# A ring of six gathered tiles instead of five, with the edges' table and early constants in the bias row's place

## The chip, the cores and the metric

The kernel runs on one core of one Trainium2 chip. The metric is the device time of one execution in microseconds, the median of several. The engines are named as in the profile: PE is TensorE, DVE is VectorE, ACT is ScalarE, POOL is GpSimd, SP is SyncE. All on-chip tensors (SBUF) have 128 partitions; PE writes into eight banks of PSUM (`ps`).

## The reference, cut to what matters

A gated relational graph layer with a normalised input, N = 1250 nodes, D = 1024 features, R = 8 relations and 20000 edges:

```python
h = jnp.maximum(_layernorm(x, axis=-1), 0.0)
# _rgcn(h, ...): msgs = h[src]
out = h @ root + bias
for r in range(8):
    mask = (edge_type == r)
    sums = segment_sum(msgs * mask[:, None], dst, num_segments=n)
    cnt = segment_sum(mask, dst, num_segments=n)
    out = out + (sums / maximum(cnt, 1.0)[:, None]) @ weight[r]
# the gate, with u = out
z = concatenate([u, h], axis=1) @ w_gate + b_gate
result = x + tanh(u) * z + h * (1.0 - z)
```

## The kernel before

The kernel multiplies first and sums afterwards. For each relation it forms y = h @ weight[r] for all nodes and stores the rows in memory off the chip (`y_rows`). Then it gathers, for each edge, the row of its source and relation, and sums the rows of the edges with the same destination by a product with a one-hot matrix. Numbers are split into a high and a low half of 16 bits, so each product of a block is three matmuls, and a row of `y_rows` holds 2 x 1024 halves (4 KB).

**The products.** All work of PE hangs on a count n of products (`for n in range(NU)`), each written to one of four banks of `ps`. The eleven weights are eight relations, root, and the two halves of w_gate. The first three take 20 products each in the plain way; from the fourth on the kernel uses seven products of quarter size for eight (`winograd(n)`, 35 per weight), and the last half of w_gate is plain again. Every engine walks through the same n in its own program, with what is due at each n written out in tables: conversions of the next weight (L765 on ACT, L1001 and L1017 on DVE), evacuations (L1123), stores and loads on SP.

**The groups and their tiles.** The edges are put into 80 groups, one for each relation and each block of 125 destinations. Early in the run (n up to 32) DVE computes each edge's place in a table of tiles of 128 edges, POOL scatters the edges into the table (L624, 160 DMAs), loads it back (L628), and DVE unpacks it into `edges` at n = 109 (`table()`). A group has at least two tiles. The groups are worked through in four sweeps, of relations 0 to 2, 3 and 4, 5 and 6, and 7. A sweep begins at a multiple of RING in the table: `group_bounds()` rounds the tiles of each sweep up to whole turns of the ring, and the last group of a sweep takes the tiles that are left over, which hold no edge. Their gathers name a row beyond the bound and move nothing.

**The ring.** `G` is a ring of RING gathered tiles of 128 x 2048 halves (4 KB per partition each), in the tensor `early`. POOL fills it. Its program for tile t is `make_onehot(t - LAG)`, then `columns(t + 1)`, then the gather of tile t (L651): the one-hot tile of t - 3 waits until that gather has landed, and the gather of t waits until PE has summed tile t - RING (`onehot_free`). So with LAG = 3 at most three gathers are in flight, and at the end of a sweep POOL makes the last three one-hot tiles (L687) before it begins the next sweep.

**The sums.** PE takes the first tile of group g at product `AGG_AT[g]` and the others one product later (`REST_AT`), from n = 113 on. A tile is four matmuls of 128x512 (L1330), for the high and low halves of both halves of the row, and one small one that counts (L1333). DVE divides the sum by the count and adds it to a block of u (`add_group`, L1202 to L1212) in one of three buffers `ub`, which SP stores to and loads from `u_rows` between sweeps. PE may begin the next group when DVE has added this one (`u_added`).

**Other places that the diff touches.** `early` also holds, at other times, the layer norm's buffers (`xbuf`, `hbuf`, `hilo`), the operand sums of the quarter-size products (`sbuf_s`, read until `s_low`), weight half C and the bias row `brow`, which DVE first reads when the root weight begins (n = 235). `weight_top` spreads a weight's maximum over 128 columns (`wspread`, L979), for PE to transpose.

## Time and profile before

| what | before |
|---|---|
| three timed runs | 1382.66, 1378.94, 1381.46 us |
| median | 1381.46 us |
| the profiled execution | 1374.83 us |
| its span | 1373.1 us |
| mean granted clock of PE | 0.989 |
| DMA, read from and written to memory | 203.66 MB and 87.30 MB |

The profile is of one execution, which is 6.63 us shorter than the median. An engine's busy time is what its instructions took; the idle time in front of an instruction is put down to the one that released it. The chain that ended last has PE for 61% of the span, DVE for 13%, DMA for 9% and issue for 9%. The first tile is summed at 501 us and the last at 1138 us.

### The profile page before, as it was taken

The page shows a single profiled execution, that of the slowest core. Times are in us where ns is not written, and L with a number is a line of the kernel's source. Part 1 is how long each engine was busy: PE and PEld are TensorE (multiplying, and loading weights), DVE is VectorE, ACT ScalarE, POOL GpSimd, SP SyncE. Part 2 cuts the span into 40 slices and gives each one's busy share as a digit, 9 for nine tenths or more (in the row PEclk, how much of TensorE's full clock was granted, in tenths as well). Part 3 has the DMA queues.
Part 4 walks back from the last instruction along what each step waited for, and adds up shares of the span by engine and source line. Part 5 has one row for each costly group of instructions (what it writes and reads, how often), then busy time and mean ns, then how long its engine had stood idle before and what let it go on. Part 6 is the DMA issues. An engine that isn't in the chain of part 4 may idle for free.

```text
span 1373.1 us, 20220 instructions
## 1 busy us (share of the span) xinstructions
PE 1280.7 (93%) x6207; PEld 646.9 (47%) x6207; DVE 953.5 (69%) x1296; ACT 425.4 (31%) x526; POOL 785.5 (57%) x880
## 2 busy tenths in 40 slices
PE   3899999999999999999998999999999889979998
PEld 1445444444444444445454445444445444434665
DVE  6879897476556747766684567556585657787886
ACT  4472223244325414320331132222311111575200
POOL 6222078787878746776787676866685644331000
PEclk9999999999999999999999999999999999998999
DMA  6371133251144268676775978588787996677876
GB/s 226 134 274 62 43 115 116 54 175 47 30 132 115 53 219 261 188 210 236 249 218 166 301 268 280 191 295 280 223 267 238 343 311 188 189 255 217 250 222 209
DMA packets 112474, 269.43 MB, mean 196 GB/s; under 512 B 22678, under 2 KB 23181, under 8 KB 112388
## 3 DMA queue, kind: packets, MB, share of 16 engines
q1 hardware_dynamic: 75204, 175.63, 38.6%
q0 software_dynamic: 37184, 92.64, 23.3%
q8 instruction: 55, 0.90, 0.3%
q14 instruction: 31, 0.25, 0.1%
HBM read 203.66 MB, written 87.30 MB: 212 GB/s over the span
## 4 chain that ended last, share of the span: by engine, by line
PE 61%; DVE 13%; DMA 9%; issue 9%; ACT 4%; POOL 3%; POOLq 0%; DVEq 0%; SPq 0%; ACTq 0%
PE ps L1368 51%; PE ps L1330 10%; DMA early<-y_rows,pair 6%; DMA early<-u_rows 2%; POOL onehot L659 2%; DVE W L1001 2%; DVE hT L1049 1%; DMA W<-in_L_gnn_weight_dram 1%; ACT W L765 1%; POOL early L651 1%; DVE wspread L979 1%; DVE yhl L1123 1%; DVE early L1212 1%; DVE yhl L1134 1%; DVE hT L1054 1%
## 5 line engine op out<-in xcount | busy, mean ns | idle before, releaser
L1368 PE MATMUL ps<-W,hT 128*128 128x512 f16 (+2 forms) x4740 | 1066.0, 382 | 12.8 <-DVE W L1001 8.2
L1368 PEld LDWEIGHTS ps<-W,hT 128*128 128x128 f16 (+2 forms) x4740 | 475.8, 103 | 528.2 <-issue 22.9
L624 POOL DMA_INDIRECT table_rows<-edges,table_i x160 | 245.3, 1533 | 112.4 <-issue 112.4
L651 POOL DMA_INDIRECT early<-y_rows,pair x200 | 234.6, 1173 | 105.3 <-PE ps L1333 62.4
L1330 PE MATMUL ps<-early,onehot 128*125 x800 | 207.6, 387 | 41.1 <-POOL onehot L659 21.6
L659 POOL TENSOR_SCALAR onehot<-iota_d,pair 128x125 f16<-128x125 f16 x188 | 152.9, 813 | 87.6 <-DMA early<-y_rows,pair 80.7
L1330 PEld LDWEIGHTS ps<-early,onehot 128*125 x800 | 106.8, 137 | 117.0 <-issue 68.2
L815 ACT ACTIVATE yhl<-early 128x512 f16<-128x512 f32 x100 | 62.8, 628 | 319.7 <-DVE early L1123 183.0
L1001 DVE SCALAR_TENSOR_TENSOR W<-W,wsc 128x2048 f16<-128x2048 f32 x62 | 148.3, 2393 | 16.4 <-ACT W L765 16.4
L765 ACT ACTIVATE W<-W,wsc 128x2048 f16<-128x2048 f32 x62 | 122.7, 1991 | 105.3 <-DVE W L1017 51.6
L732 ACT ACTIVATE peek_out<-W 128x1024 bf16<-128x1024 f32 x80 | 84.2, 1053 | 135.1 <-DMA W<-in_L_gnn_weight_dram 63.3
L1212 DVE SCALAR_TENSOR_TENSOR early<-ps,inv,early 125x1024 f32<-125x1024 f32 x70 | 89.9, 1284 | 2.4
L807 ACT ACTIVATE yhl<-ps 128x512 f16<-128x512 f32 (+1 forms) x60 | 35.7, 594 | 168.7 <-PE ps L1368 155.4
L1100 DVE SCALAR_TENSOR_TENSOR yhl<-ps,yhl 128x512 f16<-128x512 f32 (+1 forms) x60 | 40.6, 684 | 52.3 <-ACT yhl L807 45.6
L1202 DVE TENSOR_SCALAR inv<-ps,wsc 125x1 f32<-125x1 f32 x80 | 17.2, 216 | 75.8 <-PE ps L1333 65.9
L1088 DVE TENSOR_TENSOR yhl<-early,yhl 128x512 f16<-128x512 f32 x100 | 68.8, 688 | 0.7 <-ACT yhl L815 0.5
L1123 DVE SCALAR_TENSOR_TENSOR early<-ps,Q 128x512 f32<-128x512 f32 x50 | 34.5, 689 | 48.9 <-PE ps L1368 45.2
L598 POOL TENSOR_TENSOR early<-early 128x1024 f16<-128x1024 f32 (+1 forms) x10 | 27.2, 2724 | 70.8 <-ACT early L780 70.8
L1017 DVE TENSOR_TENSOR W<-W 128x2048 f32<-128x2048 f32 x26 | 61.1, 2351 | 0.1
L1123 DVE SCALAR_TENSOR_TENSOR early<-ps,hT 128x512 f32<-128x512 f32 x50 | 34.4, 689 | 36.5 <-PE ps L1368 30.5
L641 POOL COPY pair<-edges 128x2 int32 x200 | 56.5, 283 | 3.6 <-POOL onehot L687 1.9
L1123 DVE SCALAR_TENSOR_TENSOR Q<-ps,Q 128x512 f32<-128x512 f32 x50 | 34.2, 684 | 26.8 <-PE ps L1368 26.8
(191 smaller groups left out, 851.4 us busy)
## 6 DMA issues: line engine op xcount, KB each, us to landing
y_rows<-yhl SPq DMA_DIRECT2D x144, 256.0 KB
W<-in_L_gnn_weight_dram SPq DMA_DIRECT2D x30, 1024.0 KB
u_rows<-early SPq DMA_DIRECT2D x50, 448.0 KB
early<-u_rows SPq DMA_DIRECT2D x30, 448.0 KB
W<-in_L_gnn_w_gate_dram SPq DMA_DIRECT2D x8, 1024.0 KB
early<-in_x_dram SPq DMA_DIRECT2D x9, 512.0 KB, 4.8
hs_rows<-early SPq DMA_DIRECT2D x9, 512.0 KB, 4.1
root_rows<-yhl SPq DMA_DIRECT2D x18, 256.0 KB
```

The source lines that it names most:

```text
L624: pool.indirect_dma_start(out=table_rows, out_offset=bass.IndirectOffsetOnAxis(ap=at_i[:, c:c + 1], axis=0), in_=packed[0:EP, c:c + 1], in ...
L651: pool.indirect_dma_start(out=G[:, b, :], out_offset=None, in_=y_rows[i], in_offset=bass.IndirectOffsetOnAxis(ap=idx[:, b, :], axis=0), bo ...
L659: pool.tensor_scalar(onehot[:, b, 0:DT], iota_d[:, :], dcol[:, b, :], None, ALU.is_equal).then_inc(s["tile_ready"], 1)
L732: nc.scalar.activation(peek_out[:, :], homes[LAND[w][q]][:, half * D:(half + 1) * D], ACT.Abs, accum_out=wsum[:, w, 2 * q + half:2 * q + h ...
L765: nc.scalar.activation(Wv[MAT[w][c]][:, 0, :], homes[at], ACT.Copy, scale=wscale(w, 0, c // 2)).then_inc(s["w_hi"], 1)
L815: nc.scalar.activation(yhl[:, o % 4, 0, :], C[:, o % 2, :], ACT.Copy).then_inc(s["y_hi"], 1)
L1001: nc.vector.scalar_tensor_tensor(out=Wv[MAT[w][c]][:, 1, :], in0=homes[at], scalar=wscale(w, 0, c // 2), in1=Wv[MAT[w][c]][:, 0, :], op0=A ...
L1088: nc.vector.tensor_tensor(yhl[:, o % 4, 1, :], C[:, o % 2, :], yhl[:, o % 4, 0, :], ALU.subtract).then_inc(s[YDONE], 1)
L1123: return nc.vector.scalar_tensor_tensor(out=to, in0=part, scalar=scale, in1=of, op0=ALU.mult, op1=ALU.add)
L1212: nc.vector.scalar_tensor_tensor(out=ub[0:DT, b, :], in0=sums, scalar=inv[0:DT, 1:2], in1=ub[0:DT, b, :], op0=ALU.mult, op1=ALU.add).then_ ...
L1330: nc.tensor.matmul(ps[0:DT, 4 + half, :], hot_t, rows[:, bass.ds(ring_slot * (2 * D) + (half * D + part * HC), HC)], start=first and part ...
L1368: last = nc.tensor.matmul(ps[0:rows, n % 4, :], hT[:, m, v_h, k, n0:n0 + rows], Wh[MAT[w][c]][:, v_w, k, :], start=(first and v_h + v_w == ...
```

## The change

RING is 6 instead of 5, and the table is 348 columns wide instead of 345, a multiple of 6. `early` gets an eleventh block of 1024 columns, so the ring lies in blocks 1 to 6, the three buffers `ub` in blocks 7 to 9 and the bias row in block 10. The edges' table `table_i`, the group offsets `tb`, `before`, `ones_bf`, `groups`, `ltile` and `iota_g`, all of them used only before the first sweep, lie in the bias row's block until the table is unpacked. The bias row is therefore loaded at n = 133 instead of n = 10, behind a wait for `table_ready`. `ones_f` has 8 columns instead of 128, and the spread of the maximum and the helper copies at a sweep's end read other tensors. Slot 5 of the ring is cleared by a memset of its own, behind a wait for `s_low`.

```diff
--- before.py
+++ after.py
@@ -28,9 +28,9 @@
     DT = 125
     NJ = N // DT
     NG = R * NJ
-    RING = 5
+    RING = 6
     LAG = 3
-    TMAX = 345
+    TMAX = 348
     HC = 512
     HT = 5
     KH = 4
@@ -247,19 +247,21 @@
         Q = sb("Q", [P, HT, HC], F32)
         yhl = sb("yhl", [P, 4, 2, HC], F16)
         peek_out = sb("peek_out", [P, D], BF16)
-        early = sb("early", [P, 10 * D], F32)
+        early = sb("early", [P, 11 * D], F32)
         edges = sb("edges", [P, TMAX, 2], I32)
-        table_i = sb("table_i", [P, TMAX], I32)
-        tb = sb("tb", [P, NG], F32)
         ident = sb("ident", [P, P], F32)
         ident_h = sb("ident_h", [P, P], F16)
-        ones_f = sb("ones_f", [P, P], F32)
-        ones_bf = sb("ones_bf", [P, P], BF16)
-        before = sb("before", [P, P], BF16)
-        groups = sb("groups", [NG, NG + NS], BF16)
+        ones_f = sb("ones_f", [P, 8], F32)
+        at_brow = early[:, 10 * D:11 * D]
+        table_i = at_brow[:, 0:TMAX].bitcast(I32)
+        before, ones_bf, ltile = (at_brow[:, TMAX + i * P // 2:TMAX + (i + 1) * P // 2].bitcast(BF16) for i in range(3))
+        ltile = ltile[0:NG, :]
+        tb = at_brow[:, TMAX + 3 * P // 2:TMAX + 3 * P // 2 + NG]
+        groups = at_brow[0:NG, TMAX + 3 * P // 2 + NG:TMAX + 3 * P // 2 + NG + (NG + NS) // 2].bitcast(BF16)
+        iota_g = at_brow[:, TMAX + 3 * P // 2 + 2 * NG:TMAX + 3 * P // 2 + 3 * NG]
+        assert (NG + NS) % 2 == 0 and (NG + NS) // 2 <= NG and TMAX + 3 * P // 2 + 3 * NG <= D
         ones_h = sb("ones_h", [P, 2], F16)
         iota_d = sb("iota_d", [P, DT], F16)
-        iota_g = sb("iota_g", [P, NG], F32)
         pair = sb("pair", [P, RING, 2], I32)
         onehot = sb("onehot", [P, RING, P], F16)
         bounds = sb("bounds", [P, NG + 1], I32)
@@ -267,7 +269,6 @@
         turn_f = sb("turn_f", [P, 4, NS + 1], F32)
         tstart = sb("tstart", [P, NG], F32)
         ntile = sb("ntile", [NG, 4], F32)
-        ltile = sb("ltile", [NG, P], BF16)
         warm = sb("warm", [P, 1], F32)
         held = sb("held", [P, LAG * NS], F32)
         stats = sb("stats", [P, 2, 2, 6], F32)
@@ -302,9 +303,9 @@
         hbuf = early[:, 4 * D:6 * D].rearrange("p (b n) -> p b n", b=2)
         hilo = early[:, 6 * D:8 * D].bitcast(F16).rearrange("p (b n) -> p b n", b=2)
         sbuf_s = early[:, 6 * D:8 * D].rearrange("p (m k n) -> p m k n", m=4, k=KH)
-        G = early[:, D:6 * D].bitcast(F16).rearrange("p (b n) -> p b n", b=RING)
-        ub = early[:, 6 * D:9 * D].rearrange("p (b n) -> p b n", b=3)
-        brow = early[:, 9 * D:10 * D]
+        G = early[:, D:7 * D].bitcast(F16).rearrange("p (b n) -> p b n", b=RING)
+        ub = early[:, 7 * D:10 * D].rearrange("p (b n) -> p b n", b=3)
+        brow = early[:, 10 * D:11 * D]
         brow_gate = early[:, 0:D]
         uhl = [G[:, b, :] for b in (0, 1)]
         root_in = [G[:, b, :].bitcast(F32) for b in (2, 3)]
@@ -498,7 +499,8 @@
                     if r == 23:
                         sp.wait_ge(s["w_lo"], conv_no(w, 6) + 1)
                         land(w + 1, 3)
-                if n == 10:
+                if n == AGG_AT[0] + 20:
+                    sp.wait_ge(s["table_ready"], 1)
                     load_brow(brow, bias)
                 if n == unit(W_ROOT, 2, 0):
                     sp.wait_ge(s[YDONE], 2 * NJ * W_ROOT + 1)
@@ -628,8 +630,10 @@
             pool.dma_start(table_i[:, :], table_rows.rearrange("(p t) one -> p (t one)", p=P)).then_inc(s["table_loaded"], 16)
 
             pool.wait_ge(s["w_lo"], conv_no(PLAIN, 3) + 1)
+            pool.wait_ge(s["s_low"], HT)
             pool.memset(early[:, D:2 * D], 0.0).then_inc(s["ring_clear"], 1)
-            pool.wait_ge(s["ring_clear"], 2)
+            pool.memset(early[:, 6 * D:7 * D], 0.0).then_inc(s["ring_clear"], 1)
+            pool.wait_ge(s["ring_clear"], 3)
             pool.wait_ge(s["onehot_free"], RING)
             pool.wait_ge(s["tile_ready"], RING)
             pool.wait_ge(s["table_ready"], 1)
@@ -683,7 +687,7 @@
                     turn(i, q)
                 for b in range(RING - LAG, RING):
                     pool.wait_ge(s[f"gathered{b}"], q1 * 16)
-                    pool.tensor_tensor(held[:, LAG * i + b - RING + LAG:LAG * i + b - RING + LAG + 1], iota_g[:, 0:1], iota_g[:, 0:1], ALU.add)
+                    pool.tensor_tensor(held[:, LAG * i + b - RING + LAG:LAG * i + b - RING + LAG + 1], ones_f[:, 0:1], ones_f[:, 0:1], ALU.add)
                     pool.tensor_scalar(onehot[:, b, 0:DT], iota_d[:, :], dcol[:, b, :], None,
                                        ALU.is_equal).then_inc(s["tile_ready"], 1)
 
@@ -976,7 +980,7 @@
                 else:
                     dve.wait_ge(s["peeked"], 4 + 8 * w)
                     step(nc.vector.tensor_reduce(wtop[:, 0:1], wsum[:, w, :], AX.X, ALU.max))
-                nc.vector.tensor_scalar(wspread[:, :], ones_f[:, :], wtop[:, 0:1], None, ALU.mult).then_inc(s["wtop_ready"], 1)
+                nc.vector.tensor_scalar(wspread[:, :], ident[:, :], 0.0, wtop[:, 0:1], ALU.mult, ALU.add).then_inc(s["wtop_ready"], 1)
 
             def first_peek(q):
                 dve.wait_ge(s[f"w_landed{q}"], 16)
```

Two engines' orders change. On POOL, ahead of the first gather (the copy of `pair` is the last instruction before the sweeps), before:

```order
L616 MEMSET early 128x4096
L617 MEMSET onehot 128x2
L618 MEMSET onehot 128x2
L624 DMA table_rows<-edges,table_i 44160x1 x160
L628 DMA table_i<-table_rows 128x345
L631 MEMSET early 128x1024
L674 COPY pair<-edges 128x2
```

and now:

```order
L618 MEMSET early 128x4096
L619 MEMSET onehot 128x2
L620 MEMSET onehot 128x2
L626 DMA table_rows<-edges,early 44544x1 x160
L630 DMA early<-table_rows 128x348
L634 MEMSET early 128x1024
L635 MEMSET early 128x1024
L678 COPY pair<-edges 128x2
```

One memset is added ahead of the copy; the scatter and the load of the table go to `early` and have 348 columns. On SP, the bias row's load stood between the stores of the first weight's products (y_rows) and of the normalised rows (hs_rows), before:

```order
L416 DMA y_rows<-yhl 128x1024 x2
L399 DMA hs_rows<-early 128x1024
L402 DMA early<-in_L_gnn_bias_dram 128x1024
L416 DMA y_rows<-yhl 128x1024 x2
L399 DMA hs_rows<-early 98x1024
L416 DMA y_rows<-yhl 128x1024 x4
```

and now it stands between the stores of the first sweep (u_rows is the store of a finished block of sums):

```order
L417 DMA y_rows<-yhl 98x1024
L435 DMA u_rows<-early 112x1024
L435 DMA u_rows<-early 13x1024
L403 DMA early<-in_L_gnn_bias_dram 128x1024
L417 DMA y_rows<-yhl 128x1024
L435 DMA u_rows<-early 112x1024
L435 DMA u_rows<-early 13x1024
```

No other instruction of SP has moved. PE, DVE and ACT keep their order; the body of POOL's loop over the turns of the ring holds six tiles instead of five.

## Rows read from the trace of the kernel before

**Rows 1.** The page, part 1: busy us (share of span), instructions

```profile
PE 1280.7 (93%) x6207; PEld 646.9 (47%) x6207; DVE 953.5 (69%) x1296; ACT 425.4 (31%) x526; POOL 785.5 (57%) x880
```

**Rows 2.** Stretches: busy us (instructions) by engine, then granted clock, DMA share, GB/s

```profile
490.00:727.00 237.00, 226.33 (x1085) 115.26 (x1084) 159.00 (x252) 66.49 (x88) 170.85 (x227) 0.99 0.70 225
727.00:889.00 162.00, 150.46 (x721) 77.61 (x720) 99.78 (x141) 41.48 (x52) 115.24 (x160) 0.99 0.78 251
889.00:1051.00 162.00, 153.18 (x739) 78.83 (x738) 105.86 (x149) 36.83 (x42) 111.31 (x154) 0.99 0.81 258
1051.00:1139.00 88.00, 77.96 (x369) 39.57 (x368) 51.49 (x79) 15.10 (x19) 47.96 (x75) 0.98 0.94 310
```

**Rows 3.** Waits of PE, 490 to 1140 us: us, times, longest us

```profile
PE ps L1330 <- POOL onehot L659: 21.6, 19, 3.2
PE ps L1330 <- DVE early L1212: 10.6, 8, 3.9
```

**Rows 4.** Waits of POOL in the same stretch

```profile
POOL onehot L659 <- DMA early<-y_rows,pair: 80.7, 45, 5.3
POOL early L651 <- PE ps L1333: 62.4, 39, 3.3
...
POOL pair L674 <- DVE edges L1079: 8.1, 1, 8.1
```

**Rows 5.** Groups by line: the count matmul that closes each tile

```profile
L1333 PE MATMUL ps<-ones_h,onehot 128*125 128x2 f16 x200 | 33.5, 168 | 0.0
```

**Rows 6.** Timeline of PE, first to second sweep: start, us, instruction [idle before]

```profile
726.26 0.17 PE L1333 MATMUL ps<-ones_h,onehot 128*125 128x2 f16 x1
...
730.00 2.75 PE L1368 MATMUL ps<-W,hT 128*128 128x512 f16 x12
735.98 1.07 PE L1330 MATMUL ps<-early,onehot 128*125 x4 [3.23 <-POOL onehot L659]
...
738.21 1.96 PE L1330 MATMUL ps<-early,onehot 128*125 x4 [1.16 <-POOL onehot L659]
```

**Rows 7.** Timeline of PE, the ends of the second and the fourth sweep

```profile
887.49 1.06 PE L1330 MATMUL ps<-early,onehot 128*125 x4
...
889.33 5.34 PE L1368 MATMUL ps<-W,hT 128*128 128x512 f16 x24
...
1136.41 1.07 PE L1330 MATMUL ps<-early,onehot 128*125 x4
...
1137.53 1.07 PE L1330 MATMUL ps<-early,onehot 128*125 x4
```

**Rows 8.** Timeline of POOL, gathers before the first sweep's end

```profile
711.04 1.07 POOL L651 DMA_INDIRECT early<-y_rows,pair  x1 [0.62 <-POOL pair L641]
...
713.07 1.08 POOL L651 DMA_INDIRECT early<-y_rows,pair  x1 [0.16 <-issue]
...
718.36 1.07 POOL L651 DMA_INDIRECT early<-y_rows,pair  x1 [0.16 <-issue]
```

**Rows 9.** Timeline of POOL at 958 to 973 us, and of PE behind it

```profile
961.86 1.07 POOL L651 DMA_INDIRECT early<-y_rows,pair  x1 [1.48 <-PE ps L1333]
...
972.58 0.61 POOL L659 TENSOR_SCALAR onehot<-iota_d,pair 128x125 f16<-128x125 f16 x1 [5.25 <-DMA early<-y_rows,pair]
...
991.88 1.07 PE L1330 MATMUL ps<-early,onehot 128*125 x4 [2.22 <-POOL onehot L659]
```

**Rows 10.** Busy time by stretch, around one place of lower granted clock

```profile
727.00:737.00 10.00, 6.60 (x32) 3.50 (x30) 4.47 (x5) 0.63 (x1) 8.32 (x12) 1.00 0.44 119
737.00:742.00 5.00, 3.84 (x14) 1.87 (x13) 1.67 (x3) 0.00 (x0) 4.47 (x9) 0.66 0.57 177
```

**Rows 11.** Timeline, 98 to 104 us: the bias row's load

```profile
99.41 0.46 SPq L402 DMA_DIRECT2D early<-in_L_gnn_bias_dram  x1
```

**Rows 12.** Groups by line: the memset of one ring slot

```profile
L631 POOL MEMSET early<- 128x1024 f32 x1 | 1.0, 970 | 0.0
```

**Rows 13.** The instructions of L979: shortest/median/longest ns, first and last start

```profile
L979 DVE TENSOR_SCALAR wspread<-ones_f,wtop x12: 286/304/5092, 13.2 to 1231.2; 128x128 f32<-128x128 f32 x12
```

## The prediction, made before the changed kernel was run

> **What bounds the kernel now.** I read the page's busy times first, then the busy times by stretch, then the waits of PE and of POOL, and last the timeline around the ends of the sweeps. PE is busy 1280.7 us, 93% of the span of 1373.1 us [rows 1]. The stretches [rows 2] show where PE is not busy: the gathering, from 490 to 1139 us, has 649 us of which PE fills 607.9 us (226.33 + 150.46 + 153.18 + 77.96), so 41 us are idle there, and the DMA share rises from 0.70 to 0.94. In that stretch PE's idle time lies ahead of the summing matmuls of L1330 [rows 3]: 21.6 us until POOL's one-hot tile of L659, 10.6 us until DVE has added the group before (L1212). No plain product (L1368) waits there. So PE sets the time, interrupted by a ring of gathered tiles that is at times empty.
>
> Whether the ring has a slot too few is to be read from POOL [rows 4]. POOL waits 62.4 us in 39 waits for PE to free a slot (L651 on L1333), and 80.7 us in 45 waits for a gather to land (L659). Only the first kind is moved by a sixth slot. The second comes from having three gathers in flight (LAG stays 3) and from how long one takes.
>
> **Part 1, fewer tiles of nothing.** Each sweep starts on a multiple of RING, and the missing tiles are gathered, made one-hot and multiplied like real ones. All 200 show up [rows 5]. I counted the edges of the inputs by group: 71, 47, 47 and 23 real tiles in the four sweeps. Rounded to fives that is 75 + 50 + 50 + 25 = 200; rounded to sixes 72 + 48 + 48 + 24 = 192. So 8 tiles go, 3, 2, 2 and 1, each at the end of a sweep, where PE takes them one behind the other with no product between.
> - First sweep: the last padding tile that stays ends at 726.26 + 0.17 = 726.43 us, the product behind the other three starts at 730.00 us [rows 6]: 3.57 us.
> - Second: from 887.49 to 889.33 us, 1.84 us for two tiles [rows 7]. The third sweep has the same pattern, 1.84 us.
> - Fourth: one tile at the pitch from 1136.41 to 1137.53 us, 1.12 us [rows 7].
> Sum 8.4 us, all on PE, and PE has nothing beside it to hide them. The ends of the bounds: 0 if what follows each sweep waits for something else anyway, 8.4 us if not; I take 8.4 us, since the four places are solid PE.
>
> **Part 2, waits for a one-hot tile.** Of the 21.6 us [rows 3] the first tiles of the ring account for about 2.5 us: they wait for the table, not for a slot, and stay. That leaves 19.1 us.
> - At the start of the second sweep PE waits 3.23 + 1.16 = 4.39 us [rows 6]. POOL has no wait for PE between 711 and 728 us; it is busy with its own queue. From the gather at 718.36 us on, three in it are padding [rows 8], and each costs POOL at least the pitch of 2.03 us from 711.04 to 713.07 us, with its copy and its one-hot. POOL comes 6.1 us sooner, PE 3.57 us sooner, so 2.5 us of the 3.23 us go, and the 1.16 us behind it: 3.7 us. In the page this gain is not the sixth slot's but again the padding's.
> - Elsewhere one slot moves a gather that waited for PE forward by one tile of PE. From one summing to the next that is 3.48 us where one product lies between. An example [rows 9]: the gather issued at 961.86 us had waited 1.48 us for PE, and from there on POOL found no wait for PE until PE itself ran dry at 991.88 us for 2.22 us. An earlier lead of 3.48 us covers it. The other stalls outside the first sweep's end are of the same size or smaller (the longest is the 3.23 us above). I count 8.6 us for those between the ring's start and the end that stand directly behind a late one-hot tile; the other 6.1 us of the 19.1 us I leave, as waits that are put down to POOL while its tile had been ready.
> Sum 12.3 us; bounds 3.7 us (only the padding's) and 19.1 us (all).
>
> **Part 3, the clock.** The granted clock is 1.00 in the 10 us ahead of 737 us, in which PE was busy only 6.60 us, and 0.66 in the 5 us behind it [rows 10], which is a stretch at the lower level of 1.2 GHz inside one at 2.4 GHz. In it four summing matmuls took 1.96 us [rows 6], against 1.07 us in the row at 735.98 us. With the product behind them such a place costs about 1.5 us. If the wait ahead of it goes, so can this. There are three such places behind waits of the ring; I take two, 3.1 us, bounds 0 and 4.7 us.
> The Trainium skill, "TensorE: Matmul & The Clock Gate", What's actually happening, says that the clock follows how busy TensorE has been recently. The trace agrees, as far as one place shows it; by the rule all three would go, 4.7 us.
>
> **Part 4, what is given back.** The same bytes of gathers, loads and stores now fall into some 24 us less. That is 3.7% of 649 us, at a DMA share that is already 0.78 to 0.94 from 727 us on [rows 2]. The gather issued at 961.86 us had its one-hot at 972.58 us, after a wait of 5.25 us for the landing [rows 9], so within 10.7 us; 3.7% of this is 0.4 us, and I take 0.2 us as the other end, once for every three tiles in flight, so for about 41 of the 124 tiles behind the first sweep: 8 to 15 us at the worst, if every wait for landing reached PE. Most are absorbed by the ring. Bounds 0 and 15 us, I take 5 us. The bias row's load (512 KB, L402) moves from 99.41 us [rows 11] to product 133, near 570 us, where SP's queue holds it between stores and nobody is waiting for it before product 235. Its SP time is 0.46 us; its landing lies beside the gathers there. Bounds 0 and 3 us, I take 1 us. The wait for the table that now stands ahead of it on SP is over by 492 us.
>
> **Edits that I cost at nothing.** The second memset of a ring slot (0.97 us like the one before it [rows 12]) stands on POOL ahead of a wait of 8.1 us for DVE's table [rows 4]; without this cover it would cost 0.97 us. The wait for s_low in front of it is satisfied since product 56. The held copies, the smaller ones_f and the constants in the bias row keep shapes and engines. The spread of the weight maximum reads ident times 0 plus the maximum instead of ones times it: same width, one pass, 0.30 us in the median and at most 5.09 us [rows 13]. The two long ones, near 13 and 31 us, end when POOL's memsets end, whatever they read; bounds per instruction -0.05 and +0.1 us, so within 1 us for twelve.
>
> **Sum.** 8.4 + 12.3 + 3.1 - 5 - 1 = 17.8 us. The profiled execution took 1374.83 us and would take 1357 us. The median of the three timed runs is 1381.46 us, 6.6 us longer than the profiled one, and I take the sum from it: 1363.7 us.
>
> **Rivals.**
> - Only the padding goes: 8.4 + 3.7 us less, with 5 to 6 us given back: about 6 us, 1375 us. For it speaks that POOL's larger wait is for landings (80.7 against 62.4 us), which one slot doesn't shorten. Against it: after a wait for PE, each gather is issued earlier, and a lead once gained is kept until a late landing uses it.
>  The Trainium skill, "DMA: Bandwidth & Descriptors", Issuing engines are not separate DMA queues, says that all DMAs end on the same 16 engines and interleave there. By it a deeper ring buys lead and no bandwidth, so this rival's time follows. The DMA share of 0.94 [rows 2] agrees.
> - Everything that one can see goes: 8.4 + 19.1 + 4.7 us and nothing given back, 32 us; nearer to what has been seen, 27 us: 1354 us.
> - The gain is eaten behind the gathering: the last two weights, the loads of the sums or the final stage set the end by something that doesn't move with PE. Then 0 to 4 us remain, 1380 us. Against it: the chain behind 1139 us is PE and the weights' conversion, and both are released by PE's progress.
> - Slower: landings become the bound. With three in flight, each microsecond by which gathers land later delays 41 rounds, if it reaches PE. Gains of 23.8 us are used up from 0.6 us per gather on. At 0.8 us it is 33 us against 24 us, 9 us slower, 1390 us. Its place would be from 840 to 1110 us, where the DMA share is highest. Against it: the bytes don't grow, they shrink by none, and the loads keep their place in the order of products.
> - The change not doing what it says (no sixth tile, more padding) I hold excluded by the counts above.
>
> **Chances.** The forecast 0.47, only the padding 0.22, all of it 0.17, eaten behind 0.08, landings as the bound 0.06. A measurement of this kernel tells 0.3%, 4.1 us, from no change. Faster by more: 0.87 (forecast, all of it, nearly all of the padding case, and a part of the rest); within it 0.08; slower by more 0.05. The range from 1353 to 1377 us leaves out the last two cases and little else.
>
> **What would show it.** L1333 x192 instead of x200. PE's wait for L659 falls from 21.6 us to under 9 us, POOL's wait for L1333 grows, since POOL runs into the full ring more often. PE's busy time in summing falls by about 9 us. At the start of the second sweep the wait of 3.23 us is under 1 us. Fewer stretches at half clock between 490 and 1139 us. The first tile is summed at the same time, 501 us, and the gathering ends near 1120 us instead of 1139 us. It is wrong if the waits for landing (80.7 us) grow by more than the waits for a slot and PE's wait for L659 stays; if PE's wait for DVE (10.6 us) grows by 5 us or more; or if the time from the last summed tile to the end, 235 us now, becomes longer.

## The result, and the profile after

The changed kernel takes 1356.02 us in the median of four runs (1354.90 to 1360.29), the kernel before 1380.55 us (1378.94 to 1382.66) beside it. The ratio is 0.9839, 95% interval 0.9814 to 0.9864, which is 19 to 26 us less. The forecast was 1363.7 us, range 1353 to 1377: faster, as predicted, by 4 us more than the sum said when taken by the ratio (22 against 17.8 us).

The profiled execution took 1356.57 us, with a span of 1354.8 us; the one of before 1374.83 us with 1373.1 us. From one profile to the other it is 18.3 us. Part 1 of the page, to be read beside [rows 1]:

```profile
PE 1270.8 (94%) x6167; PEld 641.1 (47%) x6167; DVE 950.1 (70%) x1296; ACT 425.4 (31%) x526; POOL 775.5 (57%) x857
```

Groups by line, PE, to be read beside [rows 5]:

```profile
L1334 PE MATMUL ps<-early,onehot 128*125 x768 | 198.4, 385 | 34.1 <-DVE early L1216 13.3 <-POOL onehot L663 9.3 <-issue 7.8
L1337 PE MATMUL ps<-ones_h,onehot 128*125 128x2 f16 x192 | 32.1, 167 | 0.0
```

Lines have moved by four: L1330 is L1334 now, L1333 is L1337, L651 is L655, L659 is L663. PE counts 192 tiles. It is 9.9 us less busy, and its waits are down by 7 us. The sweeps in stretches, columns as in [rows 2]:

```profile
490.00:729.00 239.00, 228.90 (x1104) 116.65 (x1103) 162.05 (x256) 66.50 (x88) 172.82 (x232) 1.00 0.73 233
729.00:882.00 153.00, 146.70 (x711) 75.25 (x710) 101.97 (x145) 42.10 (x53) 108.88 (x146) 1.00 0.82 264
882.00:1038.00 156.00, 149.87 (x722) 76.76 (x721) 104.86 (x146) 36.21 (x42) 108.31 (x150) 0.99 0.85 269
1038.00:1122.00 84.00, 72.44 (x338) 36.71 (x337) 46.95 (x73) 15.09 (x19) 40.69 (x64) 0.96 0.91 301
```

From the first summing matmul of a sweep to that of the next, the sweeps last 225.7, 153.1, 156.3 and 84.2 us. Before, they were 234.5, 158.5, 161.2 and 82.9 us, the last one to its last tile in both. So 8.9, 5.4 and 4.9 us are gained in three sweeps, and the fourth is 1.2 us longer. This last difference tells nothing: two profiles of a ring of five, the kernel before and the first of the experiments, have 82.9 and 88.7 us there with the same 25 tiles. Outside the sweeps little moved. The first tile is summed at 502.9 us (501.4 before), and from the last tile to the end it is 232.6 us (234.5).

The waits of PE and POOL from 490 to 1125 us (us in total, times, longest us), to be read beside [rows 3, 4]:

```profile
PE ps L1334 <- DVE early L1216: 13.3, 9, 5.1
PE ps L1334 <- POOL onehot L663: 9.3, 9, 2.1
...
POOL onehot L663 <- DMA early<-y_rows,pair: 84.5, 48, 6.0
POOL early L655 <- PE ps L1337: 46.1, 27, 5.2
```

PE now waits for a one-hot tile 9 times, where it waited 19 times before (in a second profile of the same kernel, taken with the experiments, 13 times, 13.0 us). POOL waits less for PE, not more. At the start of the second sweep, where PE stood 3.23 and 1.16 us [rows 6], the timeline of PE (start, us, instruction) has no wait ahead of the first tile, and only the engine's own 0.95 us ahead of the second:

```profile
726.01 2.75 PE L1372 MATMUL ps<-W,hT 128*128 128x512 f16 x12
728.60 1.03 PE L1334 MATMUL ps<-early,onehot 128*125 x4
...
730.58 1.07 PE L1334 MATMUL ps<-early,onehot 128*125 x4 [0.95 <-issue]
```

The largest stall that is left lies in the last sweep, and it isn't the ring's. Timelines of DVE and PE there, and last the same stall of PE before the change:

```profile
1090.76 0.22 DVE L1206 TENSOR_SCALAR inv<-ps,wsc 125x1 f32<-125x1 f32 x1 [4.88 <-DMA early<-u_rows]
...
1085.04 2.75 PE L1372 MATMUL ps<-W,hT 128*128 128x512 f16 x12
1092.90 1.96 PE L1334 MATMUL ps<-early,onehot 128*125 x4 [5.11 <-DVE early L1216]
...
1108.75 1.07 PE L1330 MATMUL ps<-early,onehot 128*125 x4 [3.90 <-DVE early L1212]
```

DVE waits for the partial sums to be loaded back (u_rows), and PE waits for DVE. The tile behind it is summed at half clock (granted clock 0.50): 1.96 us in the place of 1.03. The DMA engines are nearly all busy in this stretch (third column from the end the granted clock, then their share). By windows:

```profile
1038.00:1060.00 22.00, 20.66 (x101) 10.53 (x100) 10.01 (x13) 6.20 (x9) 12.92 (x19) 1.00 0.99 322
1060.00:1080.00 20.00, 16.90 (x82) 8.29 (x79) 15.16 (x22) 2.70 (x5) 14.04 (x22) 1.00 1.00 344
1080.00:1100.00 20.00, 14.26 (x58) 6.91 (x59) 8.06 (x15) 2.30 (x4) 6.67 (x12) 0.83 0.97 336
```

### The profile page after: what moved, and what is told of

It reads as the page before. It is cut to its first block, busy times and chain, and to the rows that moved or that the text cites. A ratio compares the mean times of both kernels' runs of the same rounds, so it can differ in the third digit from the quotient of the medians.

```text
span 1354.8 us, 19982 instructions
## 1 busy us (share of the span) xinstructions
PE 1270.8 (94%) x6167; PEld 641.1 (47%) x6167; DVE 950.1 (70%) x1296; ACT 425.4 (31%) x526; POOL 775.5 (57%) x857
## 4 chain that ended last, share of the span: by engine, by line
PE 58%; DVE 13%; DMA 10%; issue 9%; ACT 4%; POOL 4%; POOLq 1%; SPq 0%; DVEq 0%; ACTq 0%
PE ps L1372 49%; PE ps L1334 9%; DMA early<-y_rows,pair 6%; POOL onehot L663 2%; DVE W L1005 2%; DMA early<-u_rows 2%; DVE hT L1053 1%; POOL early L655 1%; DMA W<-in_L_gnn_weight_dram 1%; ACT W L769 1%; DMA u_rows<-early 1%; DVE wspread L983 1%; ACT hT L847 1%; ACT peek_out L736 1%; DVE early L1216 1%
## 5 line engine op out<-in xcount | busy, mean ns | idle before, releaser
L626 POOL DMA_INDIRECT table_rows<-edges,early x160 | 248.2, 1551 | 114.6 <-issue 114.6
L655 POOL DMA_INDIRECT early<-y_rows,pair x192 | 228.7, 1191 | 86.5 <-PE ps L1337 46.1
L1334 PE MATMUL ps<-early,onehot 128*125 x768 | 198.4, 385 | 34.1 <-DVE early L1216 13.3
L663 POOL TENSOR_SCALAR onehot<-iota_d,pair 128x125 f16<-128x125 f16 x180 | 151.6, 842 | 90.1 <-DMA early<-y_rows,pair 84.5
L1005 DVE SCALAR_TENSOR_TENSOR W<-W,wsc 128x2048 f16<-128x2048 f32 x62 | 148.1, 2390 | 16.9 <-ACT W L769 16.9
L1334 PEld LDWEIGHTS ps<-early,onehot 128*125 x768 | 102.4, 137 | 107.5 <-issue 59.3
L736 ACT ACTIVATE peek_out<-W 128x1024 bf16<-128x1024 f32 x80 | 84.2, 1053 | 139.1 <-DMA W<-in_L_gnn_weight_dram 64.0
L1092 DVE TENSOR_TENSOR yhl<-early,yhl 128x512 f16<-128x512 f32 x100 | 69.1, 691 | 0.7 <-ACT yhl L819 0.5
L1021 DVE TENSOR_TENSOR W<-W 128x2048 f32<-128x2048 f32 x26 | 60.9, 2342 | 0.1
L645 POOL COPY pair<-edges 128x2 int32 x192 | 47.3, 246 | 5.1 <-issue 4.2
```

The lines of the kernel that those rows point to most:

```text
L626: pool.indirect_dma_start(out=table_rows, out_offset=bass.IndirectOffsetOnAxis(ap=at_i[:, c:c + 1], axis=0), in_=packed[0:EP, c:c + 1], in ...
L655: pool.indirect_dma_start(out=G[:, b, :], out_offset=None, in_=y_rows[i], in_offset=bass.IndirectOffsetOnAxis(ap=idx[:, b, :], axis=0), bo ...
L663: pool.tensor_scalar(onehot[:, b, 0:DT], iota_d[:, :], dcol[:, b, :], None, ALU.is_equal).then_inc(s["tile_ready"], 1)
L736: nc.scalar.activation(peek_out[:, :], homes[LAND[w][q]][:, half * D:(half + 1) * D], ACT.Abs, accum_out=wsum[:, w, 2 * q + half:2 * q + h ...
L1005: nc.vector.scalar_tensor_tensor(out=Wv[MAT[w][c]][:, 1, :], in0=homes[at], scalar=wscale(w, 0, c // 2), in1=Wv[MAT[w][c]][:, 0, :], op0=A ...
L1092: nc.vector.tensor_tensor(yhl[:, o % 4, 1, :], C[:, o % 2, :], yhl[:, o % 4, 0, :], ALU.subtract).then_inc(s[YDONE], 1)
```

## The experiments

The first theory was the prediction's: padding costs PE's time, a slot buys lead, and both add up. The rivals were that the gain comes from the layout, that the price of padding is POOL's, and that landings set the pace. Each kernel was timed in five rounds against the kernel before; the times are medians, and the ratios are to the kernel before in the same set of runs. A difference of two ratios is uncertain by about 0.004, 6 us.

### The layout and the late bias row alone

```diff
 (kernel after)
-    RING = 6
+    RING = 5
     LAG = 3
-    TMAX = 348
+    TMAX = 345
...
-        G = early[:, D:7 * D].bitcast(F16).rearrange("p (b n) -> p b n", b=RING)
+        G = early[:, D:6 * D].bitcast(F16).rearrange("p (b n) -> p b n", b=RING)
```
Everything else of the change stays, the second memset and the wait in front of it too; the block that this memset clears is then no slot of the ring.

> The changed kernel with five slots and 345 columns again; the table in the bias row's place, the bias row loaded late, the extra memset and wait, and the spread from ident all stay. My theory (fewer padding tiles and one slot more are the whole gain): 200 tiles again, 1380 us, within 0.3% of before. Rival (the table's place, the late bias row or the other small edits carry a part): clearly below 1376 us, at the extreme 1356 us.

1379.26 us beside 1379.47 us, ratio 1.0001 (0.9978 to 1.0025). The shared place, the bias row's load at product 133, the second memset and the other spread together cost and bring nothing that this can tell, that is nothing over some 3 us. So the gain is the ring's.

### Six slots, five in use

```diff
 (kernel after, gather)
-                pool.wait_ge(s["onehot_free"], t + 1)
+                pool.wait_ge(s["onehot_free"], t + 2)
```

> The changed kernel with six slots and 192 tiles, but a gather waits for one more tile to be summed, so that only five slots are ever in use. It takes the depth away and leaves the padding at 192. My theory: the padding is worth 8.4 + 3.7 = 12 us and the slot the rest, so about 1367 us (between 1363 and 1371). Rival 1 (only the padding counts): 1356 us. Rival 2 (only the slot counts): 1380 us. PE's wait for the one-hot tile: 10 to 17 us by my theory, 9 us by rival 1, 21 us by rival 2.

1367.03 us, ratio 0.9899 (0.9874 to 0.9925). With 192 tiles and the old depth 14 us are gained (10 to 17), and the sixth slot in use brings the other 8 us (0.9899 against 0.9839). The waits of PE in this kernel:

```profile
PE ps L1334 <- POOL onehot L663: 22.6, 19, 2.8
PE ps L1334 <- DVE early L1216: 9.4, 6, 3.6
```

The time is the one that my theory gave (1367 us), but the wait is not: 10 to 17 us were expected, and the 22.6 us in 19 waits are those of [rows 3], as if only the slot counted for them. Leaving out padding hardly shortens them; the slot does.

By sweep, this kernel takes 226.8, 158.7, 159.1 and 82.1 us in its profile. Against the kernel before, nearly all of the padding's gain lies in the first sweep (7.8 us for three tiles), and the two tiles that went from the second brought nothing that one profile shows; 14 us for eight tiles is an average. Against the kernel after, the sixth slot in use brings 5.5 us in the second sweep and 2.8 us in the third (5.8 us and nothing against that kernel's second profile). The start of the second sweep on PE's timeline:

```profile
729.97 1.03 PE L1334 MATMUL ps<-early,onehot 128*125 x4
...
733.76 1.07 PE L1334 MATMUL ps<-early,onehot 128*125 x4 [2.77 <-POOL onehot L663]
```

Without the padding and with the old depth the 3.23 us ahead of the first tile [rows 6] are gone, but the second tile waits 2.77 us in the place of 1.16. So 1.6 us of the 4.39 us go with the padding, and the others only with the sixth slot.

### Four slots in use

```diff
 (kernel after, gather)
-                pool.wait_ge(s["onehot_free"], t + 1)
+                pool.wait_ge(s["onehot_free"], t + 3)
```

> The kernel after (192 tiles) with gathers held back until two more slots are free, so that four of its six slots are used at a time. It draws the curve of the ring's depth at an equal number of tiles: with five of six in use the time was 1367.0, with six 1356.0 (8 to 11 us for the sixth slot). If each slot buys its 3.5 us of lead at every tile that is late, the fifth bought more than the sixth: four slots 1390 to 1415 us, ratio 1.007 to 1.025, and TensorE waits 40 to 70 us for one-hots (23 with five, 9 with six). If the gain of the sixth came by other ways (the layout, the clock), four would stand near five, 1367 to 1372 us.

1384.68 us, ratio 1.0029 (1.0008 to 1.0051). At 192 tiles the ratios for four, five and six slots in use are 1.0029, 0.9899 and 0.984: the fifth slot was worth 18 us, the sixth 8 us. The time came out under the 1390 us expected, and so did PE's wait for one-hots, 33.7 us in 34 waits and not 40 to 70 us.

### Padding tiles passed by PE, ring of five

```diff
 (kernel before, tensor engine, loop over a group's tiles)
-                with pe.Fori(t0 + 1, t1) as t:
+                with pe.Fori(t0 + 1, tr) as t:        # tr: end of the real tiles
                     sum_tile(t, False)
+                with pe.Fori(tr, t1) as t:            # padding: the counting matmul alone
+                    pass_tile(t)
```

> The kernel before, five slots and 200 tiles, but PE passes the 12 padding tiles with the small counting matmul alone, without the four summing matmuls (they add nothing to the sums). POOL still gathers and makes all 200. My theory: 12 x 0.9 us less on PE, a part of it lost because POOL's 2 us per padding tile stays and PE then waits at the start of the next sweep: 6 us less, 1374 us. Rival (a padding tile costs by PE's matmuls alone): 11 us less, 1369 us. Rival (it costs by POOL alone): no change, 1380 us.

1381.12 us, ratio 1.0003 (0.9984 to 1.0023). This told most against my theory, which had 1374 us; the rival that a padding tile costs by POOL alone had 1380 us. Some 10 us of PE's work are gone (the summing matmuls of 12 padding tiles, estimated from their 0.86 us each) and the time is the same. PE and POOL in this kernel, the same stretch:

```profile
PE ps L1333 <- POOL onehot L660: 28.9, 24, 4.6
...
POOL early L652 <- PE ps L1336: 76.7, 46, 4.0
POOL onehot L660 <- DMA early<-y_rows,pair: 64.6, 40, 6.0
```

PE waits 7.3 us more for one-hots than in [rows 3]. What it saves on padding it waits for POOL, which still has to gather it and make it one-hot.

### 24 more padding tiles

```diff
 (kernel after, group_bounds)
-    step(nc.vector.tensor_scalar(turn_f[:, 0, 0:NS], turn_f[:, 1, 0:NS], -ROUND, None, ALU.add))
+    step(nc.vector.tensor_scalar(turn_f[:, 0, 0:NS], turn_f[:, 1, 0:NS], -ROUND + 1.0, None, ALU.add))
```

> The kernel after with one more turn of its ring of six in each sweep: 24 more padding tiles, 216 tiles in all. It asks what a padding tile costs. If it is TensorE's own time, as the prediction had it, 24 x 1.05 us (the summing matmuls of one tile) = 25 us, 1381 us, ratio to the kernel before 1.002. If it is GpSimd's time, 24 x 2.04 us (gather, columns and one-hot of one padding tile) = 49 us, and nothing of it hidden, 1405 us, ratio 1.02; with the six tiles of the ring's lead hidden at each of four sweep ends, between the two. From the run with a ring of six of which five are used (8 tiles fewer than before, 13.9 us faster of 1380) I expect 1.7 us for each, 41 us: 1397 us, ratio 1.014. TensorE's wait for one-hots would rise from 9.3 us to over 25 by GpSimd's theory, and stay under 12 by TensorE's.

1404.8 us, ratio 1.0170 (1.0142 to 1.0198), against 0.984: 45 us for 24 tiles, 1.9 us each. That is near POOL's price (2.04 us), not PE's (1.05 us), with next to nothing hidden; 1397 us, 1.7 us each, had been expected. PE's wait for L663 rose to 24.5 us, just short of "over 25".

### The same, passed by PE

The edits of the last two together, on the kernel after.

> The same 216 tiles, and TensorE passes each padding tile with its counting matmul alone, so that a padding tile costs it some 0.1 us in the place of 1.05. Against the run with the 24 more padding tiles: if a padding tile's price is TensorE's work, 28 x 0.9 = 25 us of it go and the kernel is at 1355 to 1370 us; if it is GpSimd's, nothing goes (within 3 us of that run, near 1397 us) and TensorE's wait for one-hots rises by some 15 to 25 us in its place.

1406.7 us, ratio 1.0192 (1.0164 to 1.0220): nothing is gained by taking some 25 us from PE. Its waits for one-hots are 50.4 us in the place of 28.9 us with the padding summed, L691's (here L692's) included, so 21.5 us of them came back as waiting. The timelines of PE (L1346 is the counting matmul of a padding tile) and of POOL at the end of the first sweep:

```profile
727.45 0.21 PE L1346 MATMUL ps<-ones_h,onehot 128*125 128x2 f16 x1 [0.84 <-POOL onehot L664]
729.48 0.21 PE L1346 MATMUL ps<-ones_h,onehot 128*125 128x2 f16 x1 [1.82 <-POOL onehot L664]
...
725.52 1.09 POOL L656 DMA_INDIRECT early<-y_rows,pair  x1 [0.16 <-issue]
726.65 0.62 POOL L664 TENSOR_SCALAR onehot<-iota_d,pair 128x125 f16<-128x125 f16 x1
727.22 0.18 POOL L646 COPY pair<-edges 128x2 int32 x1
727.56 1.07 POOL L656 DMA_INDIRECT early<-y_rows,pair  x1 [0.17 <-POOL pair L646]
```

PE runs 0.21 us and stands 1.82 us, and its pitch of 2.03 us is that of POOL's three instructions, 1.07 to 1.09 us for the gather, 0.62 for the one-hot, 0.18 for the copy, and the gaps. Nothing of it waits for a landing here.

### Four gathers in flight

```diff
 (kernel after)
-    LAG = 3
+    LAG = 4
```

> The changed kernel with four gathers in flight instead of three (LAG 4), six slots as they are. POOL's waits for landings were 84 us in 48 waits. If they bound the gathering (the rival that landings are the bound), PE's wait for the one-hot tile falls from 9 us to under 4 us and the time by 5 us or more, under 1351 us. My theory: with six slots they are covered, the time stays within 3 us of 1356 us, and one tile less of finished lead may cost as much as it gives.

1357.04 us, ratio 0.9845 (0.9807 to 0.9882), the kernel after within its scatter. But POOL's waits change place:

```profile
POOL early L655 <- PE ps L1337: 139.5, 79, 7.2
```

In the kernel after it waited 84.5 us for landings and 46.1 us for slots. Here the one-hots wait 6.8 us for landings, and POOL waits for slots in their place. So the waits for landing are for the most part slack that shows up at one wait or the other. One reserve stays: the fourth gather in flight also means one finished tile less ahead of PE, and a gain and a loss that cancel would look the same. PE's wait for L663 hardly changed (8.6 us against 9.3).

### One more operation of GpSimd for each tile

```diff
 (kernel after, columns)
                 pool.tensor_copy(pair[:, b, :], eflat[:, bass.ds(t * 2, 2)]).then_inc(s["idx_ready"], 1)
+                pool.tensor_tensor(extra[:, b:b + 1], ones_f[:, 0:1], ones_f[:, 0:1], ALU.add)
```

The kernel after ran in the same set:

> The kernel after, unchanged, on the chip of the two kernels beside it, so that they can be read against it: 1354 to 1360 us, ratio 0.981 to 0.986.

It took 1357.75 us, ratio 0.9845 (0.9815 to 0.9875).

> The kernel after with one more operation of GpSimd for each gathered tile, an addition over one column (194 ns in the trace, some 0.25 us with its issue), behind the columns of the next tile: 192 x 0.25 = 48 us more of GpSimd's work between 490 and 1122 us. If GpSimd's own pace sets these sweeps, most of it shows: 1390 to 1404 us. If GpSimd's time counts only where no real tile is being summed (the padding tiles, 12 or so of 192, and the fill of the ring at four sweeps, 4 x 3 tiles), it is 24 x 0.25 = 6 us or less, 1356 to 1364 us, and its waits for TensorE (46 us) and for landings (84 us) shrink by what is added.

1368.83 us, ratio 0.9933 (0.9906 to 0.9960), 11 us more than the kernel after beside it. A tile takes POOL 2.21 us from gather to gather, where it took 2.04, 33 us in 192 tiles, and its busy time on the page is 34.0 us more than that of the kernel after beside it (810.1 against 776.1). Neither theory had it: a third of POOL's added time shows, where the one said nearly all and the other that of at most 24 tiles of 192. The wait that grew is PE's for the one-hot, 13.0 us in the kernel after of this set:

```profile
PE ps L1336 <- POOL onehot L665: 24.7, 16, 4.7
```

By sweep, 225.5, 157.5, 159.4 and 88.1 us stand against 225.6, 152.8, 159.3 and 83.7 us: in these two profiles the first and the third sweep hide POOL's added time, the second and the fourth don't.

### The load of u_rows one product earlier

```diff
 (kernel after, sync engine, loop over k)
+                    if n == STEP_END[k] + 1 and NJ <= k + 2 < len(STEPS):
+                        load_u(k + 2)
                     if n == STEP_END[k] + 2:
                         store_u(k)
-                        if NJ <= k + 2 < len(STEPS):
-                            load_u(k + 2)
```

> The kernel after with the load of the partial sums u_rows for a group two steps on issued one product earlier and ahead of the store that it stood behind. In the trace of the kernel after VectorE waits 4.9 us for such a load at 1090 us and TensorE 5.1 us behind it, with one stretch of 6.8 us at half clock. If SyncE's order is what makes that load late, the wait goes: 5 us of wait and up to 1.7 us of clock, 1349 to 1353 us, ratio 0.978 to 0.981 to the kernel before. If the load is late because the DMA engines are full there (0.97 to 1.00 of their time in these 60 us), the gathers land later in its place, and nothing is gained: 1355 to 1358 us, ratio 0.983 to 0.985.

1352.42 us, ratio 0.9794 (0.9762 to 0.9826), and once more, beside the kernel after:

> The kernel with the load of u_rows issued earlier once more, now beside the kernel after. Its first timing gave a ratio of 0.9794, 6 us under that of the kernel after in another set of runs, but its profile still has a wait of 6.4 us in the last sweep, on the same kind of load, and half-clock stretches in other places. If the gain is the edit's, it is again 3 to 8 us under the kernel after: 1349 to 1354 us. If it was the scatter between sets of runs, the two agree within 2 us.

1353.49 us, ratio 0.9823 (0.9790 to 0.9856), 4.3 us under the kernel after. Both sets point the same way, by 3 and 6 us by their ratios, but the intervals overlap with those of the kernel after. It is the fastest kernel here; that it beats the kernel after is likely and not shown. The times are those of my theory, but the reason that I gave fails, since the wait was to go. PE in its first profile:

```profile
1090.77 1.96 PE L1334 MATMUL ps<-early,onehot 128*125 x4 [6.37 <-DVE early L1216]
```

DVE's wait for the same kind of load is still there (4.6 us). In the second profile PE waits 6.4 us for DVE at the same place, but there the profile puts only 1.6 us of DVE's waits down to this load. That the load is late because the DMA engines are full would fit the first profile and is not shown. What shortened the second and third sweeps (by 1.9 and 3.8 us in the first profile) stays open.

### The wide operations of DVE in halves

```diff
 (the kernel with the earlier load, low_weights; sum_quadrants in the same way)
-                nc.vector.scalar_tensor_tensor(out=Wv[MAT[w][c]][:, 1, :], in0=homes[at], ...
+                for m in range(2):
+                    k = slice(m * 1024, (m + 1) * 1024)
+                    part = nc.vector.scalar_tensor_tensor(out=Wv[MAT[w][c]][:, 1, k], in0=homes[at][:, k], ...
```

> The kernel with the earlier load of u_rows, and VectorE's two widest operations on the weights (the low part L1005 and the sum of quadrants L1021, 128x2048, 2.3 us each) written as two of 1024 columns. In the trace of the kernel after, 39 gathers, one-hots and copies of GpSimd take up to 3 us in the place of 0.2 to 1.1 us while one of these runs, 50 us in all, and end a fixed 0.96, 0.48 or 0.04 us behind its end. If GpSimd is shut out until the wide operation ends, and gets in between the halves, the longest of its gathers falls from 3.1 to about 2.2 us, its lost time falls from 68 us to 35 to 45 us, and, with a third of GpSimd's time reaching TensorE as the kernel with the extra operation showed, the time falls by 8 to 11 us, to 1342 to 1346 us, ratio 0.972 to 0.975. If GpSimd does not get in between two operations that follow each other at once, the lost time stays and the time is 1351 to 1355 us, ratio 0.979 to 0.983, or 1 to 2 us more for VectorE's 100 or so added instructions.

1358.49 us, ratio 0.9849 (0.9823 to 0.9876): no gain where 8 to 11 us were expected, and some 5 us more than without the halves, about what two sets of runs can differ by. What it says of POOL stands in the last section. POOL's time lost in stretched gathers, one-hots and copies (counted there) fell by 12.7 us (67.7 to 55.0), less than expected, and nothing of that reached the end. The sweeps are as long as with whole operations (152.6 and 152.8 us for the second and third, 151.2 and 152.5 with whole ones). POOL waits 75.6 us for slots where it waited 44.0. DVE is 16 us busier, and the part behind the last tile is 4.8 us longer, 239.0 us, so this kernel doesn't tell what less contention alone is worth.

## Why the prediction was right, and where not

**What bounds the kernel.** PE's summing, interrupted by a ring that runs dry: right. The slots in use show it directly, four to six at the same tiles.

**Part 1, 8.4 us "all on PE", with "nothing beside it to hide them".** The size was near and the place wrong. Fewer padding tiles are worth 14 us (10 to 17). The prediction had 8.4 us here, 3.7 us at the second sweep's start and about 1.5 us for the clock there, 13.6 us in all. But PE's matmuls of padding are worth nothing: with them left out the time stays, in a ring of five and with 28 padding tiles in a ring of six. PE's time and POOL's are not added up at a sweep's end. PE takes the padding quickly and then waits for the next sweep's first tile, which stands behind the padding in POOL's queue. The price is 1.9 us a tile on POOL. The prediction saw that queue in [rows 8] and used it for 3.7 us only, where it should have carried the whole term: eight times 1.9 us is 15 us. Even so it is an average, since by the profiles most of it came in the first sweep.

**Part 2, one slot elsewhere 8.6 us.** Right: the step from five to six in use is 8 us, though by a difference that is itself uncertain by 6 us. The wait of PE for one-hots fell from 21.6 to 9.3 us, and to 13.0 us in the second profile, against "under 9". The 3.7 us at the second sweep's start were put down to the padding alone; with six slots, five in use, only 1.6 us of them came, and the others with the sixth slot.

**Part 3, the clock, 3.1 us.** Before, four stretches at half clock lay between 490 and 1139 us, 3.4 us long each. In the profile after there are two, 3.4 us at 885.9 us and 6.8 us at 1090.7 us, 10.2 against 13.6 us, and a new one of 3.4 us stands at 145.2 us, behind a wait of PE of 2.93 us for DVE that has nothing to do with the ring. The fall at 737.7 us is gone, as predicted. Half a clock over 3.4 us is 1.7 us, so by this profile 1.7 us came back in the sweeps, half of the term, and nothing in the whole. But the second profile of the same kernel has 13.6 us at half clock in the sweeps again (885.6, 977.8 and 1093.8 us). So the runs don't show the term at all.

**Part 4, given back 5 us and 1 us.** The bias row's 1 us was 0 within what the first experiment can tell. The 5 us for denser DMA were laid on landings, and there they did not show: the waits for landing rose by 3.8 us (80.7 to 84.5), and four gathers in flight, which took them away, changed nothing. The last sweep is 1.2 us longer and PE's wait for DVE in all sweeps 13.3 us where it was 10.6, but two profiles of a ring of five have 10.6 and 13.0 us too. So no run shows that anything was given back. The measured parts, 14 us for the padding and 8 us for the slot, add up to the 22 us by themselves. The 4 us between them and the sum of 17.8 us are, as far as the runs tell, what was taken off here for nothing.

**The starting point.** From profile to profile the sum of 17.8 us met 18.3 us. The 1363.7 us were 7.7 us too high. The timed medians fell by 24.5 us, more than the two profiles did. The profiled run of before, 1374.83 us, was a short one among runs from 1372 to 1385 us.

**The rivals.** "Only the padding", 1375 us, falls: the padding was worth more, and the slot came on top. "Slower, landings the bound" falls with the time itself. "Eaten behind the gathering" falls, since the tail is 1.9 us shorter. "All of it", 1354 us, came nearest to the measured 1356 us. It had all waits gone (9.3 us stayed) and nothing given back.

**The checks.** The 192 tiles, PE's summing 9.2 us less busy (207.6 to 198.4 us), the start of the second sweep and the end of the gathering (1122 us) came as said. "POOL's wait for L1333 grows" was wrong: it fell from 62.4 to 46.1 us. With 192 tiles and four, five and six slots in use it was 115.2, 61.7 and 46.1 us: a ring with more slots is less often full. The first check to drop next time is a wait of an engine that has slack.

## What to carry to other kernels

A padding or empty step cost here what the slower stage of its queue spends on it, not what the last stage spends, where the next sweep's tiles stood behind it; read the producer's pitch at the place where the consumer next runs dry. A ring's slots are best measured at constant work, by making the producer wait for one or two more free slots: it is one number in one line, it takes apart depth and the padding that changes with it, and the curve (18, then 8 us) helps to judge whether another is worth it. Waits of an engine with slack can move from one semaphore to the next and prove nothing by themselves; change what they wait for and look at the time.

## What the runs showed of the hardware

GpSimd's instructions stretch while DVE runs a wide operation with two inputs in SBUF. In the kernel after, 53 of the gathers, one-hots and copies take over 0.3 us more than their usual 1.08, 0.63 and 0.19 us, 71 us in sum. 40 of them overlap with such an operation of 2048 columns, the other 13 with one of 512 columns (12 with L1092, one with L1138). Timelines of POOL and DVE at 878 us, and of PE behind them:

```profile
878.58 3.12 POOL L655 DMA_INDIRECT early<-y_rows,pair  x1 [0.24 <-issue]
881.74 2.81 POOL L663 TENSOR_SCALAR onehot<-iota_d,pair 128x125 f16<-128x125 f16 x1
...
878.40 2.34 DVE L1005 SCALAR_TENSOR_TENSOR W<-W,wsc 128x2048 f16<-128x2048 f32 x1
...
881.86 2.28 DVE L1021 TENSOR_TENSOR W<-W 128x2048 f32<-128x2048 f32 x1
...
884.86 1.07 PE L1334 MATMUL ps<-early,onehot 128*125 x4 [2.09 <-POOL onehot L663]
```

The gather ends 0.96 us behind the end of L1005, the one-hot 0.4 us behind that of L1021, and PE, with nothing in the ring, waits 2.09 us. Over the 40 the distance to the end of the wide operation has a median of 0.96 us for a gather, 0.48 for a one-hot and 0.04 for a copy, so the end is tied to DVE's end and not to the instruction's own start. Which of the two starts first matters too. 15 gathers overlap with a wide operation by over 0.2 us and keep their usual length: 14 of them had begun 0.05 to 0.86 us ahead of it, one 8 ns behind. The 11 stretched ones had all begun 0.14 us or more behind its start. For one-hots the line is less sharp: three of the 24 stretched ones had begun up to 0.12 us ahead. DVE's operations take 2.28 to 2.35 us in either case. With the operations in halves the longest gather falls from 3.12 us (3.20 in the kernel with the earlier load alone) to 2.08 us (shortest/median/longest ns):

```profile
L655 POOL DMA_INDIRECT early<-y_rows,pair x192: 1011/1084/2077, 497.7 to 1102.6; - x192
```

That is 1.0 us less, about what a half is shorter than the whole (1.34 and 1.25 us against 2.39 and 2.34). One such gather in this kernel, and the two halves of L1026 (x2) beside it:

```profile
580.00 1.96 POOL L655 DMA_INDIRECT early<-y_rows,pair  x1 [0.25 <-issue]
...
579.79 2.35 DVE L1026 TENSOR_TENSOR W<-W 128x1024 f32<-128x1024 f32 x2
```

The gather ends at 581.96 us, while the second half still runs, and 0.94 us behind the end of the first, which is at 581.01 us. So GpSimd gets in between two operations of DVE that follow each other at once, which I had not been sure of. The Trainium skill, "SBUF — State Buffer", Who interferes with whom, says that a VectorE instruction with two SBUF inputs contends with a GpSimd instruction that reads SBUF, and that the port pair which the two engines share is an exclusive lock. The stretched instructions agree: all 53 overlap with such an instruction of VectorE. What it costs this kernel is not shown: 12.7 us of POOL's time came back and the time did not fall, but DVE had more work by the same edit.

A gather costs POOL the same whether its rows are real or all out of bounds: 1.09 and 1.07 us for the padding tiles at 725.52 and 727.56 us above, against a median of 1.08 us over all 192 gathers of the kernel after.
